# Who asks for the adapters: moving a layer's small loads from SyncE's queue to GpSimd's, and four row buffers used in turn

## The chip, the cores and the metric

The kernel runs on one core of a Trainium2 chip. Its metric is the device time of one execution in microseconds (us), taken as the median of several runs. The core has five engines with instruction streams of their own: TensorE (PE) multiplies and transposes, VectorE (DVE) and ScalarE (ACT) work element by element, GpSimd (POOL) and SyncE (SP) here mostly ask for transfers. Each stream runs in order; an instruction waits until its semaphores have the values that it names. A transfer is asked for by an engine's queue (SPq, POOLq, ACTq) and carried out by 16 DMA engines that all queues share.

## The reference

Four layers with residual connections follow each other on x, 64 sequences of 32 tokens of 512 features (2048 rows in all):

```python
x = x + L0(x, weight[ids0])                        # a 512x512 matrix chosen per sequence
x = x + (x @ W1.T + b1 + scale * (x @ A1[id].T) @ B1[id].T)   # 8 adapters of rank 16
x = x + (x @ W2.T + b2 + 2 * (x @ A2[id]) @ B2[id])           # 32 adapters of rank 16
x = x + attention(x)                               # QKV, norm, rope, paged cache, projection
```

All arithmetic is float32. The change touches only how the two middle lines (the low-rank layers) get their data.

## The kernel before

The stages run one behind another: layer 0, the two low-rank layers (`lora_layers`), QKV and attention, output projection. Every product is made in three passes over a high and a low part of each operand (L102 to L104), so each operand is split: ScalarE writes the high part, VectorE subtracts it to get the low part.

`lora_layers` holds the activations transposed (features on partitions). The 2048 rows are 16 tiles of 128 rows (`NT`), in four groups of four tiles (`LG`, `TPG`). Each of the two layers is applied to each group in a round; the eight rounds go in the order `ROUNDS` (layer, group): (0,0) (0,1) (1,0) (0,2) (1,1) (0,3) (1,2) (1,3). A round on TensorE is `low_rank` (the product with A), then four times `base` (with W) and `delta` (with B), one for each 128 output features. Ahead of each of the four `base` steps there may be one turn, four transposes of 128x128 (L798): in rounds 0, 2 and 4 an input tile of the next group ("x"), in rounds 3, 5 and 7 a finished tile ("z"), which ScalarE copies to a row buffer and SP stores.

A round of layer 1 needs the eight-sequence adapters of its group: for each half of a group, eight A matrices (128 partitions of 64 numbers, 32 KB) to `a_in` and eight B matrices (16 rows of 512 numbers, 32 KB) to `b_in`, each by a DMA of its own whose address comes from a register. That is 32 DMAs for a group. There is one `a_in` and one `b_in` buffer for each half, so a group's load has to wait until the group before has been split. The split of A is done one round ahead, at its head (`a_hi_part` on ScalarE, L654, then `a_lo_part` on VectorE, L741), before that round's additions (`add`, L728) on VectorE and their splits; that of B at the round's end (`b_hi_part` L662, `b_lo_part` L749).

SP asks for all of it in one written order: input tiles (`load_x`, L564), small constants, W2 (L592), the adapters (`load_adapters`, L576 and L578) and the stores (L583). In its loop over the groups the load of the adapters stands between the first two and the last two input tiles of a group:

```python
if g:
    sp.wait_ge(ab_split, 4 * g)
```

Input tile t goes to row buffer t for the first four tiles, then to buffer 0 or 1 alone (`x_buf`), since buffers 2 and 3 take the finished tiles. GpSimd does nothing in this stage.

Of the kernel before, what the change touches and what calls it, by code (L numbers as in the profile page):

```python
# [25 lines left out]
P = 128  # L26
NSEQ, SEQ, D = 64, 32, 512
TOK = NSEQ * SEQ
NT = TOK // P
SPT = P // SEQ  # L30
KC = D // P
NAD0 = 8
NAD1, NAD2, RANK = 8, 32, 16
# [423 lines left out]
LG = 4  # L457
GT = TOK // LG
TPG = NT // LG
HS = P // RANK  # L460
HT = HS * SEQ
ROUNDS = [(0, 0), (0, 1), (1, 0), (0, 2), (1, 1), (0, 3), (1, 2), (1, 3)]
ROUND_OF = {step: n for n, step in enumerate(ROUNDS)}
# [6 lines left out]
TURN_OF = {turn: n for n, turn in enumerate(TURNS)}  # L470


def lora_layers(nc, place, both, kept, a_in, b_in, weights_loaded, x_in, i, x_out, w_next):
# [9 lines left out]
    with ExitStack() as ctx:  # L483
        m = Mem(nc, ctx, "lora")
        w_hi, w_lo = low_part.sb("w_hi", [P, 2, KC, D], fp32r), low_part.sb("w_lo", [P, 2, KC, D], fp32r)
        state = [low_part.sb(f"state{n}", [P, KC, GT]) for n in range(2)] + [kept.w_stage[:, 1, :, :]]
# [8 lines left out]
        x_sb = high_part.sb("x", [P, 4, D])  # L495
        ids_f, ids2_sb = high_part.sb("ids_f", [P, NSEQ]), high_part.sb("ids2", [1, NSEQ], i32)
# [5 lines left out]
        small_loaded, ids2_loaded, mask_chain = m.sem("small_loaded"), m.sem("ids2_loaded"), m.sem("mask_chain")  # L502
        weights_hi, weights_split = m.sem("weights_hi"), m.sem("weights_split")
        x_loaded, turned = m.sems("x_loaded", 4), m.sem("turned")
        x_hi_done, x_split, z_copied = m.sem("x_hi_done"), m.sem("x_split"), m.sem("z_copied")
        ab_loaded, ab_hi_done, ab_split = m.sems("ab_loaded", 2), m.sem("ab_hi_done"), m.sem("ab_split")
        low_done, masked = m.sem("low_done"), m.sem("masked")
        low_hi_done, low_split = m.sem("low_hi_done"), m.sem("low_split")
        mm_done, y_ready, y_hi_done, y_split = m.sem("mm_done"), m.sem("y_ready"), m.sem("y_hi_done"), m.sem("y_split")
# [3 lines left out]
        A1, W1, B1, W2 = range(4)  # L513
        FIRST_OF = {A1: 0, W1: 1, B1: 1 + KC, W2: 2 + KC}
        PIECES_SPLIT = 2 + 2 * KC

        def pieces(which):
# [5 lines left out]
                return [(b_in[:, 1, :], b1_hi[:, :], b1_lo[:, :])]  # L523
            l = 0 if which == W1 else 1
            return [(w_in[:, l, k, :], w_hi[:, l, k, :], w_lo[:, l, k, :]) for k in range(KC)]

        def x_buf(t):
            return t if t < 4 else t % 2

        def x_loads(t):  # L530
            return 1 if t < 4 else (t - 4) // 2 + 2

        def tokens(g):
            return slice(g * GT, (g + 1) * GT)
# [1 line left out]
        def rows(t):  # L536
            return slice(t * P, (t + 1) * P)

        def in_group(t):
            return slice(t % TPG * P, (t % TPG + 1) * P)  # L540
# [12 lines left out]
        def adapters_after(n):  # L553

            step = ROUNDS[n + 1] if n + 1 < len(ROUNDS) else (0, 0)
            return step[1] if step[0] else None

        with nc.Block(no_gpsimd_drain=True) as block:
            @block.sync
            def _(sp):  # L560
                def load_x(t):
                    if t >= 4:
                        sp.wait_ge(turned, TURN_OF["x", t - 4 if t < 6 else t - 2] + 1)
                    sp.dma_start(x_sb[:, x_buf(t), :], x_in[rows(t), :]).then_inc(x_loaded[x_buf(t)], 16)  # L564

                def load_adapters(g):
                    for h in range(2):
                        _, adapters = nc.values_load_multi_w_load_instructions(
                            ids2_sb[0:1, (2 * g + h) * HS:(2 * g + h + 1) * HS], engines=[mybir.EngineType.SP],
                            min_val=0, max_val=NAD2 - 1, skip_runtime_bounds_check_because="ids are adapters")  # L570
                        if g:
                            sp.wait_ge(ab_split, 4 * g)
                        elif h:
                            sp.wait_ge(weights_split, FIRST_OF[W2])
                        for s, a in enumerate(adapters):
                            sp.dma_start(a_in[:, h, s * KC * RANK:(s + 1) * KC * RANK], i["a2"][bass.ds(a, 1)])\  # L576
                              .then_inc(ab_loaded[h], 16)
                            sp.dma_start(b_in[s * RANK:(s + 1) * RANK, h, :], i["b2"][bass.ds(a, 1)])\  # L578
                              .then_inc(ab_loaded[h], 16)

                def store(t):
                    sp.wait_ge(z_copied, t + 1)
                    sp.dma_start(x_out[rows(t), :], x_sb[:, 2 + t % 2, :]).then_inc(both.x_stored[t % 2], 16)  # L583

                for t in range(TPG):
                    load_x(t)
                for buf, src in smalls:
                    sp.dma_start(buf[:, :], src).then_inc(small_loaded, 16)
                sp.dma_start(ids2_sb[:, :], i["ids2"]).then_inc(ids2_loaded, 16)
                for t in range(TPG, TPG + 2):  # L590
                    load_x(t)
                sp.dma_start(w_in[:, 1, :, :], i["w2"]).then_inc(weights_loaded[W2], 16)  # L592
                sp.wait_ge(ids2_loaded, 16)
                load_adapters(0)
                for t in range(TPG + 2, TPG + 4):
                    load_x(t)
                sp.wait_ge(weights_split, FIRST_OF[B1])
                sp.dma_start(w_in[:, 0, :, :], w_next).then_inc(kept.w_loaded[0], 16)
                for g in range(1, LG):
                    if g < LG - 1:  # L600
                        for t in range(TPG * (g + 1), TPG * (g + 1) + 2):
                            load_x(t)
                    load_adapters(g)
                    if g < LG - 1:
                        for t in range(TPG * (g + 1) + 2, TPG * (g + 2)):
                            load_x(t)
                    for t in range(TPG * (g - 1), TPG * g):
                        store(t)
                for t in range(NT - TPG, NT):
                    store(t)  # L610

            @block.scalar
            def _(act):
# [33 lines left out]
                    act.activation(hi, state[g % 3][:, c, :], ACT.Copy).then_inc(y_hi_done, 1)  # L647

                def a_hi_part(g):
                    for h in range(2):  # L650
                        act.wait_ge(ab_loaded[h], 16 * 2 * HS * (g + 1))
                        if g:
                            act.wait_ge(low_done, ROUND_OF[1, g - 1] + 1)
                        act.activation(a2_hi[:, h, :, :].rearrange("p k (s r) -> p s k r", s=HS),  # L654
                                       a_in[:, h, :].rearrange("p (s k r) -> p s k r", s=HS, k=KC), ACT.Copy)\
                           .then_inc(ab_hi_done, 1)

                def b_hi_part(g):
                    if g:
                        act.wait_ge(mm_done, KC * (ROUND_OF[1, g - 1] + 1))  # L660
                    for h in range(2):
                        act.activation(b2_hi[:, h, :], b_in[:, h, :], ACT.Copy).then_inc(ab_hi_done, 1)  # L662
# [13 lines left out]
                for n in range(len(ROUNDS)):  # L676
                    g = adapters_after(n)
                    low_hi_part(n)
                    turn(n, 0)
                    if g is not None:  # L680
                        a_hi_part(g)
                    for c in range(KC):
                        y_hi_part(n, c)
                        if c + 1 < KC:
                            turn(n, c + 1)
                        if n == 0 and c == 0:
                            split_weights_hi(W2)
                    if g is not None:
                        b_hi_part(g)
# [96 lines left out]
            def _(pe):  # L786
                def transpose(kind, t):
                    turn = TURN_OF[kind, t]
                    if turn >= 2:
                        last_kind, last_t = TURNS[turn - 2]  # L790
                        pe.wait_ge(x_split if last_kind == "x" else z_copied, last_t + 1)
                    if kind == "x":
                        pe.wait_ge(x_loaded[x_buf(t)], 16 * x_loads(t))
                    else:
                        pe.wait_ge(y_ready, KC * (ROUND_OF[1, t // TPG] + 1))
                    for k in range(KC):
                        src = x_sb[:, x_buf(t), k * P:(k + 1) * P] if kind == "x" else state[t // TPG % 3][:, k, in_group(t)]
                        last = pe.transpose(ps_t[:, turn % 2, k, :], src, ident[:, :])  # L798
                    last.then_inc(turned, 1)

# [52 lines left out]
                def turn(n, at):  # L853
                    kind, t = turn_in(n, at)
                    if kind:
                        transpose(kind, t)

                pe.wait_ge(ident_ready, 1)
                for t in range(TPG):
                    transpose("x", t)  # L860
# [6 lines left out]
                for t in range(NT - TPG, NT):  # L867
                    transpose("z", t)
# [1127 lines left out]
```

## Time and profile before

| | |
|---|---|
| median of 3 runs | 2545.6 us (2545.35 to 2546.51) |
| profiled execution, its own time | 2544.21 us |
| its span, first to last instruction | 2542.6 us |
| mean granted TensorE clock | 0.976 |
| PE, DVE, ACT, POOL busy share of the span | 95%, 70%, 63%, 24% |
| low-rank stage, by the timeline | about 106 to 318 us |

The span is the length of the profiled execution without what lies ahead of its first and behind its last instruction, here 1.6 us. Times in the trace count from the start of the span. A busy share is a mean over stages that have different limits.

### The profile page before, as it was taken

To read this page: it belongs to the slowest core of one execution; us is meant where nothing else is said; L and a number is where in the kernel's file an instruction comes from. 1 tells how busy PE (TensorE), PEld (TensorE's weight loads), DVE (VectorE), ACT (ScalarE), POOL (GpSimd) and SP (SyncE) were. 2 spreads that over 40 slices of the span, in tenths; PEclk is the share of its full clock that TensorE was granted. 3 is DMA by queue.
4 is the path that set the end of the run, shared out by engine and by line. 5 is a ranking of instruction groups with operands and counts; after the bars stand their busy time and mean duration, and the time that the engine had idled before them with its cause. 6 is when DMAs were issued, how large, how long until landed. Compare 5 with 4: busy or idle time off the path is not lost. (4 is left out here: it accounts for less than half of the span.)

```text
span 2542.6 us, 54643 instructions
## 1 busy us (share of the span) xinstructions
PE 2409.0 (95%) x16070; PEld 2195.2 (86%) x16071; DVE 1780.3 (70%) x3632; ACT 1602.2 (63%) x3311; POOL 599.9 (24%) x896
## 2 busy tenths in 40 slices
PE   6878799999999979999999999999999997699999
PEld 4656688888888869999999999999999997588887
DVE  5434334989998977888878878788788884544443
ACT  3223235877777778888888888888888884311111
POOL 1200012000000024444444444444544442000000
PEclk9889999999999989999999999999999999799999
DMA  6521132333333469888888898888888884766664
GB/s 221 174 64 55 61 140 88 103 100 113 99 100 99 133 192 302 291 295 297 303 281 304 285 294 303 282 300 293 292 301 281 299 276 161 273 206 213 210 213 148
DMA packets 373752, 536.83 MB, mean 211 GB/s; under 512 B 49314, under 2 KB 263010, under 8 KB 369826
## 3 DMA queue, kind: packets, MB, share of 16 engines
q1 hardware_dynamic: 301538, 311.62, 38.2%
q0 software_dynamic: 70016, 221.30, 25.6%
q10 hardware_dynamic: 2112, 2.89, 0.4%
q8 instruction: 38, 0.62, 0.1%
q14 instruction: 48, 0.39, 0.0%
HBM read 437.35 MB, written 98.30 MB: 211 GB/s over the span
## 5 line engine op out<-in xcount | busy, mean ns | idle before, releaser
L1669 PE MATMUL both_ps_o<-att_pt,att_v 128*128 128x128 f32 x4096 | 539.3, 275 | 0.0
L1367 ACT ACTIVATE att_prob<-att_prob,att_shift 128x544 f32<-128x544 f32 x512 | 384.4, 751 | 205.5 <-DVE att_shift L1387 195.8
L1669 PEld LDWEIGHTS both_ps_o<-att_pt,att_v 128*128 128x128 f32 x4096 | 504.0, 191 | 0.0
L1387 DVE CUSTOM_DVE_ANT_0 att_prob<-both_ps_s,att_mask 128x544 f32<-128x544 f32 x512 | 365.0, 713 | 0.0
L102 PE MATMUL both_ps_s<-att_k_hi,att_q_hi 128*128 128x272 f32 x1024 | 339.2, 331 | 4.8 <-DVE att_k_lo L1362 4.8
L1362 DVE TENSOR_TENSOR att_k_lo<-att_k_raw,att_k_hi 128x1024 fp32r<-128x1024 f32 (+1 forms) x320 | 338.6, 1058 | 1.9 <-ACT att_k_hi L1356 1.9
L1646 PE MATMUL both_ps_pt<-both_ident,att_prob 128*128 128x128 f32 x2048 | 309.2, 274 | 7.8 <-ACT att_prob L1367 6.2
L104 PE MATMUL both_ps_s<-att_k_hi,att_q_lo 128*128 128x272 f32 x1024 | 298.0, 291 | 0.0
L1545 ACT ACTIVATE att_pt<-both_ps_pt 128x512 f32<-128x512 f32 x512 | 294.3, 575 | 2.2 <-PE both_ps_s L1654 1.2
L103 PE MATMUL both_ps_s<-att_k_lo,att_q_hi 128*128 128x272 f32 x1024 | 295.3, 288 | 0.0
L1356 ACT ACTIVATE att_k_hi<-att_k_raw 128x1024 fp32r<-128x1024 f32 (+1 forms) x320 | 292.7, 915 | 0.0
L1487 POOL DMA_INDIRECT att_v<-in_v_pages,att_rows_now x256 | 252.5, 986 | 86.1 <-issue 86.1
L1481 POOL DMA_DIRECT2D att_vo<-v_own x256 | 139.7, 546 | 555.1 <-PE both_ps_o L1672 494.0
L1577 DVE TENSOR_REDUCE att_p_own<-att_prob 128x32 f32<-128x32 f32 x512 | 91.0, 178 | 236.0 <-PE both_ps_s L104 222.0
L1646 PEld LDWEIGHTS both_ps_pt<-both_ident,att_prob 128*128 128x128 f32 x2048 | 242.4, 142 | 8.5 <-ACT att_prob L1367 6.5
L1823 ACT ACTIVATE out_o_hi<-out_o 128x2048 fp32r<-128x2048 f32 x32 | 61.4, 1918 | 290.3 <-DVE out_o L1850 282.5
L102 PE MATMUL out_ps_y<-out_w_hi,out_o_hi 128*128 128x512 f32 x512 | 202.9, 396 | 36.5 <-DVE out_w_lo L1843 31.0
L103 PE MATMUL out_ps_y<-out_w_lo,out_o_hi 128*128 128x512 f32 x512 | 202.1, 395 | 0.0
L104 PE MATMUL out_ps_y<-out_w_hi,out_o_lo 128*128 128x512 f32 x512 | 201.9, 394 | 0.0
L102 PEld LDWEIGHTS both_ps_s<-att_k_hi,att_q_hi 128*128 128x128 f32 x1024 | 194.7, 190 | 6.9 <-DVE att_k_lo L1362 5.2
L1672 PE MATMUL both_ps_o<-att_pto,att_vo 128*128 128x128 f32 x1024 | 198.0, 275 | 0.0
L103 PEld LDWEIGHTS both_ps_s<-att_k_lo,att_q_hi 128*128 128x128 f32 x1024 | 195.9, 191 | 0.0
(209 smaller groups left out, 5036.0 us busy)
## 6 DMA issues: line engine op xcount, KB each, us to landing
att_k_raw<-in_k_pages SPq DMA_DIRECT2D x1024, 128.0 KB, 4.8
q_t<-qkv_out_t SPq DMA_DIRECT2D x128, 256.0 KB, 2.3
att_q_raw<-q_t POOLq DMA_DIRECT2D x64, 512.0 KB, 7.5
o_t<-att_o POOLq DMA_DIRECT2D x64, 512.0 KB, 7.0
out_o<-o_t SPq DMA_DIRECT2D x32, 1024.0 KB, 6.0
out_inv<-inv_t SPq DMA_DIRECT2D x32, 1024.0 KB, 6.6
both_w_stage<-in_w_qkv SPq DMA_DIRECT2D x12, 1024.0 KB, 5.2
l_w_stage<-in_w SPq DMA_DIRECT2D x8, 1024.0 KB, 7.4
```

What stands on the lines that cost most here:

```text
L102: pe.matmul(out, xh, wh, start=start, stop=False)
L103: pe.matmul(out, xh, wl, start=False, stop=False)
L104: return pe.matmul(out, xl, wh, start=False, stop=stop)
L1356: act.activation(hi, raw, ACT.Copy).then_inc(hi_done, 1)
L1362: dve.tensor_tensor(lo, raw, f32(hi), ALU.subtract).then_inc(lo_done, 1)
L1367: act.activation(prob[:, b, :], prob[:, b, :], ACT.Exp, bias=shift[:, b:b + 1], scale=-1.0, accum_out=total[:, j // HK, j % HK:j % HK + 1] ...
L1387: dve.tensor_tensor_reduce(out=prob[:, b, :].rearrange("p (a n) -> p a n", a=2), in0=ps_s[:, j % 2, :, 0:HALF], in1=mask[:, j // HK, :].re ...
L1487: pool.indirect_dma_start(v_sb[p][:, c, :], None, v_pages.rearrange("n k x -> (n k) x"), bass.IndirectOffsetOnAxis(ap=rows_now[:, p, c:c + ...
L1545: act.activation(pt_sb[:, j % OG, :, :], ps_pt[:, j % 2, :, :], ACT.Copy).then_inc(pt_ready, 1)
L1646: mm = pe.transpose(ps_pt[:, j % 2, c, :], prob[:, j % NB_P, c * P:(c + 1) * P], ident[:, :])
L1669: pe.matmul(out, v_sb[p][:, c, h * DH:(h + 1) * DH], pt_sb[:, j % OG, c, :], start=(c == 0), stop=False)
L1672: pe.matmul(out, vo_sb[p][:, g % 2, j % OG, :], pto_sb[:, g % 2, :], start=False, stop=True).then_inc(pv_done, 1)
```

## The change

- The loads of the adapters go from SP's stream to GpSimd's. For a group they are in four lots: A of half 0, B of half 0, A of half 1, B of half 1, with eight DMAs in each.
- Each lot waits only for the split of what it overwrites: `ab_split` counts A0, A1, B0, B1 of a group, and the lots of group g wait for 1, 3, 2 and 4 of the group before. Before, both halves waited for all four.
- There is one semaphore for all A loads and one for all B loads. `a_hi_part` now waits ahead of its first half for all sixteen A loads of its group, and for no B load; `b_hi_part` waits for the B loads.
- Input tiles use all four row buffers in turn. Tile t waits until tile t-4 has been transposed. The last two (14 and 15) go to the buffers that finished tiles 0 to 3 have passed through and wait for those stores.
- On SP, W2 now stands behind input tiles 4 to 7; before, it stood behind 4 and 5. Tiles 8 to 11 are asked for before the first QKV weights.

```diff
-                        sp.wait_ge(turned, TURN_OF["x", t - 4 if t < 6 else t - 2] + 1)
-                    sp.dma_start(x_sb[:, x_buf(t), :], x_in[rows(t), :]).then_inc(x_loaded[x_buf(t)], 16)
+                        sp.wait_ge(turned, TURN_OF["x", t - 4] + 1)
+                    if t >= NT - 2:
+                        sp.wait_ge(both.x_stored[t % 2], 16 * 2)
+                    sp.dma_start(x_sb[:, t % 4, :], x_in[rows(t), :]).then_inc(x_loaded[t % 4], 16)
...
-                for t in range(TPG, TPG + 2):
+                for t in range(TPG, 2 * TPG):
                     load_x(t)
                 sp.dma_start(w_in[:, 1, :, :], i["w2"]).then_inc(weights_loaded[W2], 16)
-                sp.wait_ge(ids2_loaded, 16)
-                load_adapters(0)
-                for t in range(TPG + 2, TPG + 4):
+                for t in range(2 * TPG, 3 * TPG):
                     load_x(t)
                 sp.wait_ge(weights_split, FIRST_OF[B1])
                 sp.dma_start(w_in[:, 0, :, :], w_next).then_inc(kept.w_loaded[0], 16)
-                for g in range(1, LG):
-                    if g < LG - 1:
-                        for t in range(TPG * (g + 1), TPG * (g + 1) + 2):
-                            load_x(t)
-                    load_adapters(g)
-                    if g < LG - 1:
-                        for t in range(TPG * (g + 1) + 2, TPG * (g + 2)):
-                            load_x(t)
-                    for t in range(TPG * (g - 1), TPG * g):
-                        store(t)
+                for t in range(3 * TPG, NT - 2):
+                    load_x(t)
+                for t in range(TPG):
+                    store(t)
+                for t in range(NT - 2, NT):
+                    load_x(t)
+                for t in range(TPG, NT - TPG):
+                    store(t)
                 for t in range(NT - TPG, NT):
                     store(t)
+            @block.gpsimd
+            def _(pool):
+                def load_adapters(g):
+                    for h in range(2):
+                        _, adapters = nc.values_load_multi_w_load_instructions(
+                            ids2_sb[0:1, (2 * g + h) * HS:(2 * g + h + 1) * HS], engines=[mybir.EngineType.Pool],
+                            min_val=0, max_val=NAD2 - 1, skip_runtime_bounds_check_because="ids are adapters")
+                        if g:
+                            pool.wait_ge(ab_split, 4 * (g - 1) + h + 1)
+                        elif h:
+                            pool.wait_ge(weights_split, FIRST_OF[W2])
+                        for s, a in enumerate(adapters):
+                            pool.dma_start(a_in[:, h, s * KC * RANK:(s + 1) * KC * RANK], i["a2"][bass.ds(a, 1)])\
+                                .then_inc(a_loaded, 16)
+                        if g:
+                            pool.wait_ge(ab_split, 4 * (g - 1) + 2 + h + 1)
+                        for s, a in enumerate(adapters):
+                            pool.dma_start(b_in[s * RANK:(s + 1) * RANK, h, :], i["b2"][bass.ds(a, 1)])\
+                                .then_inc(b_loaded, 16)
+
+                pool.wait_ge(ids2_loaded, 16)
+                for g in range(LG):
+                    load_adapters(g)
...
                 def a_hi_part(g):
+                    act.wait_ge(a_loaded, 16 * 2 * HS * (g + 1))
+                    if g:
+                        act.wait_ge(low_done, ROUND_OF[1, g - 1] + 1)
                     for h in range(2):
-                        act.wait_ge(ab_loaded[h], 16 * 2 * HS * (g + 1))
...
                 def b_hi_part(g):
+                    act.wait_ge(b_loaded, 16 * 2 * HS * (g + 1))
```

## Rows read from the trace of the kernel before

**Rows 1.** Busy us by engine (x instructions) in the low-rank and the attention stage.
```profile
core 0: us, PE busy (x) PEld busy (x) DVE busy (x) ACT busy (x) POOL busy (x), PEclk, DMA share, GB/s
106.00:318.00 212.00, 162.41 (x800) 135.55 (x800) 84.21 (x125) 64.19 (x116) 0.00 (x0) 0.88 0.24 70
...
830.00:2260.00 1430.00, 1377.31 (x11193) 1342.44 (x11192) 1117.42 (x2517) 1101.93 (x2144) 551.47 (x835) 0.98 0.82 272
```

**Rows 2.** PE's timeline, turns only: start, duration, instruction, idle before and its releaser.
```profile
112.24 2.10 PE L798 MATMUL lora_ps_t<-both_ident,lora_x 128*128 128x128 f32 x8 [1.05 <-DVE both_xt_lo L703]
...
124.36 0.60 PE L798 MATMUL lora_ps_t<-both_ident,lora_x 128*128 128x128 f32 x4
...
133.91 1.08 PE L798 MATMUL lora_ps_t<-both_ident,lora_x 128*128 128x128 f32 x4 [5.46 <-DMA lora_x<-x]
...
140.47 0.60 PE L798 MATMUL lora_ps_t<-both_ident,lora_x 128*128 128x128 f32 x4
...
167.99 0.60 PE L798 MATMUL lora_ps_t<-both_ident,lora_x 128*128 128x128 f32 x4
...
184.28 1.09 PE L798 MATMUL lora_ps_t<-both_ident,lora_x 128*128 128x128 f32 x4 [12.20 <-DMA lora_x<-x]
...
189.69 0.60 PE L798 MATMUL lora_ps_t<-both_ident,lora_x 128*128 128x128 f32 x4
...
215.00 0.60 PE L798 MATMUL lora_ps_t<-both_ident,lora_x 128*128 128x128 f32 x4
...
218.94 0.60 PE L798 MATMUL lora_ps_t<-both_ident,lora_x 128*128 128x128 f32 x4
...
234.78 1.09 PE L798 MATMUL lora_ps_t<-both_ident,lora_x 128*128 128x128 f32 x4 [11.75 <-DMA lora_x<-x]
...
240.50 0.60 PE L798 MATMUL lora_ps_t<-both_ident,lora_x 128*128 128x128 f32 x4
...
293.10 1.08 PE L798 MATMUL lora_ps_t<-both_ident,both_w_stage 128*128 128x128 f32 x4 [4.09 <-DVE both_w_stage L728]
```

**Rows 3.** SP's timeline: W2, group 1's first adapter, input tiles 10 and 11.
```profile
111.64 0.43 SPq L592 DMA_DIRECT2D both_w_stage<-in_w  x1
...
164.87 0.34 SPq L576 DMA_DIRECT2D lora_a_in<-in_a  x1
...
181.44 0.88 SPq L564 DMA_DIRECT2D lora_x<-x  x2
```

**Rows 4.** ACT's timeline: the splits of W2 and of the adapters' A.
```profile
126.84 2.19 ACT L617 ACTIVATE lora_w_hi<-both_w_stage 128x512 fp32r<-128x512 f32 x4
...
148.60 1.14 ACT L654 ACTIVATE lora_a_hi<-lora_a_in 128x512 fp32r<-128x512 f32 x2
...
198.34 1.14 ACT L654 ACTIVATE lora_a_hi<-lora_a_in 128x512 fp32r<-128x512 f32 x2
...
284.79 0.63 ACT L654 ACTIVATE lora_a_hi<-lora_a_in 128x512 fp32r<-128x512 f32 x1 [8.07 <-DMA lora_b_in<-in_b]
```

**Rows 5.** DVE's timeline: B's split of groups 0 and 2, then the late addition.
```profile
163.42 1.29 DVE L749 TENSOR_TENSOR lora_b_lo<-lora_b_in,lora_b_hi 128x512 fp32r<-128x512 f32 x2
...
265.17 1.29 DVE L749 TENSOR_TENSOR lora_b_lo<-lora_b_in,lora_b_hi 128x512 fp32r<-128x512 f32 x2
...
286.06 0.74 DVE L728 SCALAR_TENSOR_TENSOR both_w_stage<-lora_ps_y,lora_bias,both_w_stage 128x512 f32<-128x512 f32 x1
```

**Rows 6.** POOL's DMA groups in the whole trace: total us, mean ns of one.
```profile
L1469 POOL DMA_DIRECT2D att_k_raw<-k_own x64 | 35.4, 553 | 57.7 <-DMA k_own<-qkv_out_t 57.5
...
L229 POOL DMA_DIRECT2D x<-l_y x44 | 22.0, 501 | 80.5 <-DVE l_y L390 78.8
```

**Rows 7.** POOL's timeline in layer 0: two stores, two register loads ahead of them.
```profile
58.41 1.08 POOL L229 DMA_DIRECT2D x<-l_y  x2 [1.33 <-DVE l_y L390]
```

**Rows 8.** DMA issues in three stretches: count, KB each, median us to landing.
```profile
both_w_stage<-in_w SPq DMA_DIRECT2D x1, 1024.0 KB, 8.8
...
lora_a_in<-in_a SPq DMA_DIRECT2D x16, 32.0 KB, 1.7
...
att_k_raw<-k_own POOLq DMA_DIRECT2D x1, 128.0 KB, 4.5
```

More of the change, by code:

```diff
@@ L505, in lora_layers @@
         x_hi_done, x_split, z_copied = m.sem("x_hi_done"), m.sem("x_split"), m.sem("z_copied")
-        ab_loaded, ab_hi_done, ab_split = m.sems("ab_loaded", 2), m.sem("ab_hi_done"), m.sem("ab_split")
+        a_loaded, b_loaded, ab_hi_done, ab_split = m.sem("a_loaded"), m.sem("b_loaded"), m.sem("ab_hi_done"), m.sem("ab_split")
         low_done, masked = m.sem("low_done"), m.sem("masked")
@@ L525, in pieces @@
             return [(w_in[:, l, k, :], w_hi[:, l, k, :], w_lo[:, l, k, :]) for k in range(KC)]
[L527 to L531, printed above, removed]
         def tokens(g):
@@ L562, in load_x @@
                     if t >= 4:
-                        sp.wait_ge(turned, TURN_OF["x", t - 4 if t < 6 else t - 2] + 1)
-                    sp.dma_start(x_sb[:, x_buf(t), :], x_in[rows(t), :]).then_inc(x_loaded[x_buf(t)], 16)
[L566 to L579, printed above, removed]
+                        sp.wait_ge(turned, TURN_OF["x", t - 4] + 1)
+                    if t >= NT - 2:
+                        sp.wait_ge(both.x_stored[t % 2], 16 * 2)
+                    sp.dma_start(x_sb[:, t % 4, :], x_in[rows(t), :]).then_inc(x_loaded[t % 4], 16)
                 def store(t):
@@ L649, in a_hi_part @@
                 def a_hi_part(g):
+                    act.wait_ge(a_loaded, 16 * 2 * HS * (g + 1))
+                    if g:
+                        act.wait_ge(low_done, ROUND_OF[1, g - 1] + 1)
                     for h in range(2):
-                        act.wait_ge(ab_loaded[h], 16 * 2 * HS * (g + 1))
-                        if g:
-                            act.wait_ge(low_done, ROUND_OF[1, g - 1] + 1)
                         act.activation(a2_hi[:, h, :, :].rearrange("p k (s r) -> p s k r", s=HS),
@@ L792, in transpose @@
                     if kind == "x":
-                        pe.wait_ge(x_loaded[x_buf(t)], 16 * x_loads(t))
+                        pe.wait_ge(x_loaded[t % 4], 16 * (t // 4 + 1))
                     else:
@@ L796, in transpose @@
                     for k in range(KC):
-                        src = x_sb[:, x_buf(t), k * P:(k + 1) * P] if kind == "x" else state[t // TPG % 3][:, k, in_group(t)]
+                        src = x_sb[:, t % 4, k * P:(k + 1) * P] if kind == "x" else state[t // TPG % 3][:, k, in_group(t)]
                         last = pe.transpose(ps_t[:, turn % 2, k, :], src, ident[:, :])
```

## The prediction

> **What bounds the kernel now.** I read the page first, then busy time by stage, then PE's timeline through the stage that the diff touches, and last SP, ACT and DVE around each gap found there. TensorE is busy for 95% of the span, but not in every stage: in the low-rank stage it works for 162.4 of 212 us, at a mean granted clock of 0.88 [rows 1]. So there are 50 us of idle time, and some work at the lower level of the clock (1.2 instead of 2.4 GHz). Only this stage can change; what comes behind it depends on its end and moves with it.
>
> PE's timeline shows where the time goes. Turns that find their tile ready come every 3.94 us (215.00 to 218.94). Three do not: tiles 6, 10 and 14, at 133.91, 184.28 and 234.78, each behind an idle time that the load of an input tile ends [rows 2]. SP's timeline says why: the first of group 1's 32 adapter DMAs goes out at 164.87, tile 10's load at 181.44 [rows 3]. SP spends 16.6 us on asking, and the tile stands behind it although its buffer was free earlier. A fourth gap has another form: the turn at 293.10 waits for an addition on VectorE [rows 2]. Round 6's additions start at 286.06 [rows 5], because the split of group 3's A stands ahead of them and the second half's arrives only at 284.79 [rows 4].
>
> **What goes: three stalls on input tiles.** I take start to start over two turns, so that the low clock after the stall is counted. At pace two turns need 7.88 us.
> - Tile 6: 140.47 - 124.36 - 7.88 = 8.2 us.
> - Tile 10: 189.69 - 167.99 - 7.88 = 13.8 us.
> - Tile 14: 240.50 - 218.94 - 7.88 = 13.7 us [rows 2].
>
> In each the idle time is 5.5, 12.2 and 11.8 us, the rest (2.6, 1.5, 1.8 us) is the turn and the base step behind it at the low clock: a turn lasts 1.08 us instead of 0.60 [rows 2]. What is late next? Without the stall of tile 6, the split of W2 (ACT from 126.84, 2.19 us [rows 4]) pushes tile 7's split to about 136.3, where the next low-rank product wants it at 136.15. I take off 0.2: 8.0 us. The other two leave nothing behind: their tiles are now loaded when tiles 6 and 7 are turned, some 30 us ahead, and, for 14 and 15, when the stores of tiles 2 and 3 have landed, near 191 on the new clock of the stage, against a need near 201. Sum: 8.0 + 13.8 + 13.7 = 35.5 us.
>
> **What is added: 128 DMAs on GpSimd's queue.** It is idle in this stage [rows 1], so the asking is free as long as the data comes in time. Three unknowns:
> - Spacing s of two DMAs. A 128-row load takes POOL 0.55 us, a 32-row store 0.50, and a pair of stores with register addresses 1.08 [rows 6, 7]. I take 0.62, with some register arithmetic. Bounds: 0.50 and, as on SP for A and B alike, 0.52 (16.6 / 32) are at the low end; at the high end I use 0.75, twice the arithmetic.
> - R, eight register loads. Two fit into 1.33 us of idle time [rows 7], so R is under 5.3; SP's whole lot of 16.6 us holds two such sets beside 32 DMAs, so it is likely under 1. I take 0.8, bound 2.
> - L, from asking to landing. SP's A load lands after 1.7 us; the one POOL load of 128 rows in a quiet stretch, four times as large, after 4.5 [rows 8]. I take 3.5, between these bounds and nearer to the POOL row.
>
> A sentence beside these: the Trainium skill ("DMA: Bandwidth & Descriptors", Latency and other measured facts) gives about 1 us to the first byte for a GpSimd DMA against 0.6 for SP's. By that alone L would be near 2.1 and the sum 1.4 us better; no row here shows it for this transfer.
>
> Each group wants its A before `a_hi_part`. The last A load is the sixteenth DMA counted from B0's start, which waits for the B0 split of the group before. So A is complete 15 s + R + L = 9.3 + 0.8 + 3.5 = 13.6 us after that split.
> - Group 0: POOL starts near 113.5 (W2's request at 111.64 [rows 3] and a small load's landing); 23 s + 2 R + L = 19.4 us later it is 132.9. Wanted at 148.60 - 8.0 = 140.6 [rows 4]. Hidden by 7.7.
> - Group 1: the split ends at 163.42 + 0.65 - 8.0 = 156.1 [rows 5]; wanted at 198.34 - 21.8 = 176.5 [rows 4]. Budget 20.4 against 13.6. Hidden by 6.8. Group 2 has the same distances.
> - Group 3: here there is no round between. The split ends at 265.17 + 0.65 = 265.8 [rows 5], A is complete at about 279.5 (old clock of the stage), and ACT has long been waiting. From the split's start to the first addition are then 1.9 us, both halves in a row. So the addition comes at 281.4 instead of 286.06 [rows 5]: 4.7 us gained, and the turn at 293.10 moves with it. PE still idles over 4 us there, so I count no gain of clock.
>
> The B loads end eight DMAs later and are wanted a round later: hidden.
>
> **What moves.** W2 is asked for behind tiles 6 and 7, which wait for the turns of tiles 2 and 3 (until 114.3 [rows 2]): some 3 us later than 111.64. It took 8.8 us [rows 8], so it lands near 123.6, with half a megabyte more ahead of it perhaps 124.5; its split starts at 126.84 [rows 4]. Hidden by 2 us; if that cover goes, each microsecond costs one. Tiles 14 and 15 behind stores, and stores behind tile loads, cost nothing (above; ACT waits for a store only two tiles on).
>
> **Sum.** 35.5 + 4.7 = 40.2 us. The profiled execution took 2544.2 us (span 2542.6), 1.4 below the median of 2545.6. It would take 2504.0; the median 2505.4. I say 2505.5. All tests below use 5 us (0.2%) as what a measurement of this kernel tells from no change.
>
> **The rivals.**
> 1. *The last gap closes further.* POOL is quick (s 0.54, R 0.6, L 1.7): A of group 3 arrives 10.4 us after the split instead of 13.6, 3.2 us more gained, and PE's idle time there may be too short for the clock to fall, 1.7 more. Gain 45, time 2500.5. For it: the pair of 1.08. Against it: the 4.5 us. It is inside my range; 0.08 for gains beyond 44.
> 2. *POOL's DMAs wait for VectorE.* The mechanism: a DMA on POOL cannot go on while a VectorE operation runs. VectorE makes 125 operations in 84.2 us here [rows 1], 0.67 us each. If each DMA waits for a whole one, s = 1.29. Then group 0's A (23 s) is late beyond s = 0.96 and groups 1 and 2 (15 s) beyond 1.07, so the gain is 103.7 - 68 s = 16 us, the time about 2529.5. Against it: in the attention stage VectorE is busy for 1117 of 1430 us [rows 1] and POOL's loads still take 0.55 [rows 6]. I give 0.06. The Trainium skill ("SBUF — State Buffer", Who interferes with whom) states a rule of this kind: a VectorE instruction with two SBUF inputs keeps out a GpSimd one that reads SBUF, for its whole length. The subtractions of L736 and L749 are of that form; by the attention stage's rows the trace does not show it for DMAs.
> 3. *POOL becomes the bound (the other side).* The same sum reaches zero at s = 1.53: all four groups' A late, group 0 by 13 us, groups 1 and 2 by 7 each, group 3's gain turned into a loss of 9. Then slower than before above s = 1.6; at s = 1.8 the time is 2564. It needs a DMA to cost three times what any direct POOL row shows; many small pieces (A has 128 of 256 bytes) would be the reason. 0.04.
> 4. *The change doesn't reach what PE waits for:* tiles 6, 10 and 14 are late for another reason, such as the shared DMA engines being full. They are busy for 0.24 of the stage [rows 1]. Time 2545.6. 0.02.
>
> **How the numbers follow.** Forecast (gain 33 to 44): 0.80; rival 1 0.08, rival 2 0.06, rival 3 0.04, rival 4 0.02. The forecast's own ends: the slow ends of s, R and L together (0.75, 2, 4.5) put A of group 3 at 17.8 us after the split, 4.2 later than taken, and W2 late by 2 more makes 6: 2511.5. The quick ends make 2500.5. With the small rest of rival 2 the range of 8 in 10 is 2499 to 2514. Faster by over 0.2%: 0.94; within: 0.02; slower: 0.04.
>
> **What the new profile would show.** Turns of tiles 6, 10 and 14 without idle time and 0.60 us long; PE's busy time in the stage near 157 us in a stretch of 172. SP with single tile loads right behind the turns. POOL with lots of eight DMAs; their spacing is s, the last A of group 3 to ACT's L654 is L. ACT's L654 waiting in group 3 alone. The turn of tile 8's result still behind idle time that VectorE ends. The prediction is wrong if L654 waits in group 0, 1 or 2 (s over 0.96), if VectorE's operations grow longer beside POOL's DMAs, if the W2 split (L617) waits, or if a tile turn waits for a load again.

## The result, and the profile after

| | before | after |
|---|---|---|
| median of 4 runs | 2546.06 us (2545.35 to 2548.94) | 2504.11 us (2501.86 to 2507.69) |
| profiled execution, its span | 2544.21, 2542.6 us | 2502.53, 2501.0 us |
| ratio | | 0.9834, 95% interval 0.9817 to 0.9851 |

The forecast was 2505.5 us, with 2499 to 2514 as its range; 2504.1 lies 1.4 below it. The span is 41.6 us shorter.

The windows view of the kernel after, in the low-rank stage (the columns are those of [rows 1]):
```profile
106.00:276.40 170.40, 155.79 (x800) 130.36 (x800) 83.82 (x124) 63.29 (x115) 65.77 (x128) 0.94 0.28 87
```
It answers to the first of [rows 1]. The stage ends 41 us sooner with the same 800 matmuls. PE is busy for 6.6 us less, since fewer of them ran at the low clock (mean 0.94 instead of 0.88), and POOL now works for 65.8 us.

PE's timeline of the kernel after, turns of tiles 5, 6, 7, 10, 11, 14, 15 and of tile 8's result:
```profile
125.90 0.60 PE L800 MATMUL lora_ps_t<-both_ident,lora_x 128*128 128x128 f32 x4
129.84 0.60 PE L800 MATMUL lora_ps_t<-both_ident,lora_x 128*128 128x128 f32 x4
133.78 0.60 PE L800 MATMUL lora_ps_t<-both_ident,lora_x 128*128 128x128 f32 x4
...
165.37 0.60 PE L800 MATMUL lora_ps_t<-both_ident,lora_x 128*128 128x128 f32 x4
169.32 0.60 PE L800 MATMUL lora_ps_t<-both_ident,lora_x 128*128 128x128 f32 x4
...
202.51 0.60 PE L800 MATMUL lora_ps_t<-both_ident,lora_x 128*128 128x128 f32 x4
206.46 0.60 PE L800 MATMUL lora_ps_t<-both_ident,lora_x 128*128 128x128 f32 x4
...
252.25 1.08 PE L800 MATMUL lora_ps_t<-both_ident,both_w_stage 128*128 128x128 f32 x4 [3.40 <-DVE both_w_stage L730]
```
The idle times of 5.46, 12.20 and 11.75 us before tiles 6, 10 and 14 [rows 2] are gone: these turns come 3.94 us behind the one before and last 0.60 us. Against the same turns of [rows 2], tile 7's is 6.7 us earlier (140.47 to 133.78), tile 11's 20.4, tile 15's 34.0, and that of tile 8's result 40.9 (293.10 to 252.25). So the three stalls and the last gap gave 6.7, 13.7, 13.7 and 6.8 us. The remaining 0.7 us of the span lie behind that turn, 0.3 of them still in this stage.

The last gap is smaller but there. ACT's timeline of the kernel after, the splits of W2 and of group 3's A:
```profile
128.38 2.19 ACT L618 ACTIVATE lora_w_hi<-both_w_stage 128x512 fp32r<-128x512 f32 x4
...
243.32 1.15 ACT L655 ACTIVATE lora_a_hi<-lora_a_in 128x512 fp32r<-128x512 f32 x2 [9.61 <-DMA lora_a_in<-in_a]
```
DVE's, the split of group 2's B and the first addition of round 6:
```profile
231.16 1.29 DVE L751 TENSOR_TENSOR lora_b_lo<-lora_b_in,lora_b_hi 128x512 fp32r<-128x512 f32 x2
...
245.20 0.75 DVE L730 SCALAR_TENSOR_TENSOR both_w_stage<-lora_ps_y,lora_bias,both_w_stage 128x512 f32<-128x512 f32 x1
```
POOL's, the lots B0 and A1 of group 3 between them:
```profile
232.13 4.06 POOL L606 DMA_DIRECT2D lora_b_in<-in_b  x8 [10.39 <-DVE lora_b_lo L751]
237.21 4.63 POOL L601 DMA_DIRECT2D lora_a_in<-in_a  x8 [1.02 <-issue]
```
ScalarE waits 9.6 us for A. The lot B0 waits for VectorE's split, A1 waits behind B0, ScalarE for A1, and the additions stand behind the split. From the first half of the B split (231.8) to the addition it is 13.4 us; before it was 20.2 [rows 5].

### The profile page after: what moved, and what is told of

It is laid out like the page before. It is cut to its first block and busy times, and to the rows that moved or that the text cites. A ratio compares the mean times of both kernels' runs of the same rounds, so it can differ in the third digit from the quotient of the medians.

```text
span 2501.0 us, 54645 instructions
## 1 busy us (share of the span) xinstructions
PE 2403.6 (96%) x16070; PEld 2190.7 (88%) x16071; DVE 1779.8 (71%) x3632; ACT 1601.7 (64%) x3311; POOL 663.3 (27%) x1024
```

## The experiments

The kernels ran in three batches, each batch on one chip beside the kernel before. Medians in us:

| batch | kernel | median | less than before |
|---|---|---|---|
| 1 | before | 2641.6 | |
| 1 | r_after, the changed kernel | 2601.6 | 40.0 |
| 1 | e_sp_asks | 2600.8 | 40.8 |
| 1 | e_two_bufs | 2600.5 | 41.1 |
| 1 | e_order_only | 2607.3 | 34.3 |
| 2 | before | 2547.2 | |
| 2 | e_a_first | 2499.0 | 48.2 |
| 2 | e_sp_a_first | 2497.2 | 50.0 |
| 2 | e_cut2 | 2519.8 | 27.4 |
| 2 | e_cut4 | 2665.8 | -118.6 |
| 3 | before | 2547.4 | |
| 3 | r_after2, the changed kernel | 2504.3 | 43.1 |
| 3 | e_wait_all | 2509.7 | 37.6 |
| 3 | e_two_bufs_w2 | 2511.7 | 35.6 |
| 3 | e_sp_a_first2 | 2498.4 | 49.0 |

The executions of one kernel in a batch spread over 1.4 to 6 us (11.6 in e_sp_a_first), so differences of medians under 2 us say nothing. Batch 1's chip is slower for every kernel; the expectations' absolute times are those of the other two chips, so there the last column is to be compared (the changed kernel's is 40 to 43). One of the six executions of e_two_bufs took 7369.7 us, which no row explains; it doesn't matter to the median.

**The base lines, r_after and r_after2.** The changed kernel, unedited.

> The changed kernel once more, as the base line of this chip for the runs beside it. Both theories: 2504 us (measured 2504.1).

> The changed kernel, as the base line of this chip for the runs beside it: 2504 us where the kernel before takes 2546.

It gains 40.0 and 43.1 us: ratios 0.9846 (0.9833 to 0.9858) and 0.9833 (0.982 to 0.9847).

**Is it GpSimd's queue, or the order? e_sp_asks.** GpSimd's block goes; SP gets the same lots with the same waits. The function `load_adapters`, which goes over with SP in GpSimd's place, is left out here:
```diff
+                sp.wait_ge(ids2_loaded, 16)
+                load_adapters(0)
                 for t in range(2 * TPG, 3 * TPG):
                     load_x(t)
...
+                load_adapters(1)
                 for t in range(3 * TPG, NT - 2):
                     load_x(t)
                 for t in range(TPG):
                     store(t)
                 for t in range(NT - 2, NT):
                     load_x(t)
+                load_adapters(2)
                 for t in range(TPG, 2 * TPG):
                     store(t)
+                load_adapters(3)
                 for t in range(2 * TPG, NT - TPG):
                     store(t)
...
-            @block.gpsimd
...
```


> The changed kernel, but SP asks for the adapters again, in the new order: each group's adapters behind the input tiles that are wanted before them, in lots A0, B0, A1, B1, with the new waits and four row buffers. Theory 1 (TensorE waited only for the place of the tile loads in one queue; any queue that brings the data in time will do): no tile turn waits; group 3's A is complete 8 + 0.8 + 1.7 = about 10.5 us after the B split (SP's spacing of about 0.5), against 11.5 on GpSimd: 2503 us, within 2 of the changed kernel. Theory 2 (a queue of its own for the adapters is what helps; SP cannot carry both in time): at least one tile turn waits again or a store holds the copies up, 5 to 25 us more: 2509 to 2530.

The same time within noise, 0.9 us below r_after. SP's timeline, group 3's lots A0, B0 and A1:
```profile
228.78 4.00 SPq L572 DMA_DIRECT2D lora_a_in<-in_a  x8
232.90 3.90 SPq L577 DMA_DIRECT2D lora_b_in<-in_b  x8
237.53 3.99 SPq L572 DMA_DIRECT2D lora_a_in<-in_a  x8
```
SP asks every 0.5 us, no slower than GpSimd, and no tile turn waits. Theory 2 falls: GpSimd's queue is one way to get the order, and not needed for it.

**The order alone, in the kernel before: e_order_only.** Two row buffers, one queue, the wait for all four splits.
```diff
-                sp.wait_ge(ids2_loaded, 16)
-                load_adapters(0)
                 for t in range(TPG + 2, TPG + 4):
                     load_x(t)
+                sp.wait_ge(ids2_loaded, 16)
+                load_adapters(0)
...
-                        for t in range(TPG * (g + 1), TPG * (g + 1) + 2):
+                        for t in range(TPG * (g + 1), TPG * (g + 2)):
                             load_x(t)
                     load_adapters(g)
-                    if g < LG - 1:
-                        for t in range(TPG * (g + 1) + 2, TPG * (g + 2)):
-                            load_x(t)
```


> The kernel before with one edit: the four input tiles of a group are asked for ahead of the adapters in SP's order; two buffers, SP alone, the wait for all four splits. Theory 1: tiles 6, 10 and 14 no longer wait (35.5 us gained), but SP waits for the turn of the fourth tile before it starts on the adapters, so the A of groups 0, 1 and 2 comes about 2 us later than ScalarE wants it (5 to 7 us in all if nothing covers it), and group 3's gap stays: 2546 - 29 = 2517 us, 2510 to 2520. Theory 2 (a queue of its own is needed): little gained, over 2530.

34.3 of the 40.0 us, where I had expected 29. ACT's timeline of this run, A's second half in groups 0, 1, 2 and 3:
```profile
144.18 0.63 ACT L651 ACTIVATE lora_a_hi<-lora_a_in 128x512 fp32r<-128x512 f32 x1 [3.06 <-DMA lora_b_in<-in_b]
...
180.88 0.63 ACT L651 ACTIVATE lora_a_hi<-lora_a_in 128x512 fp32r<-128x512 f32 x1 [3.84 <-DMA lora_b_in<-in_b]
...
217.07 0.63 ACT L651 ACTIVATE lora_a_hi<-lora_a_in 128x512 fp32r<-128x512 f32 x1 [2.89 <-DMA lora_b_in<-in_b]
...
249.27 0.63 ACT L651 ACTIVATE lora_a_hi<-lora_a_in 128x512 fp32r<-128x512 f32 x1 [8.11 <-DMA lora_b_in<-in_b]
```
In this kernel one semaphore counts the A and the B loads of a half, so the split of A waits for both. In groups 0 to 2 they are late by 2.9 to 3.8 us, as thought, but PE has no idle time in those rounds: it goes on in the open round meanwhile. A wait of ScalarE is not yet a wait of TensorE. Group 3's gap stays whole: PE idles 4.81 us ahead of the last low-rank product and 3.98 ahead of the turn of tile 8's result, where the kernel before idles 4.80 and 4.09 and the changed kernel only 3.49 in all (r_after, on the same chip). That is the difference to the changed kernel.

**Are the four buffers needed? e_two_bufs and e_two_bufs_w2.** Both use the old buffers for input tiles. The first also has W2 back ahead of tiles 6 and 7; the second leaves it behind them: of the diff it has only the first part, up to the first "...". The two functions for the buffer numbers and the reading side on PE, both as in the kernel before, are left out.
```diff
-                        sp.wait_ge(turned, TURN_OF["x", t - 4] + 1)
-                    if t >= NT - 2:
-                        sp.wait_ge(both.x_stored[t % 2], 16 * 2)
-                    sp.dma_start(x_sb[:, t % 4, :], x_in[rows(t), :]).then_inc(x_loaded[t % 4], 16)
+                        sp.wait_ge(turned, TURN_OF["x", t - 4 if t < 6 else t - 2] + 1)
+                    sp.dma_start(x_sb[:, x_buf(t), :], x_in[rows(t), :]).then_inc(x_loaded[x_buf(t)], 16)
...
-                for t in range(TPG, 2 * TPG):
+                for t in range(TPG, TPG + 2):
                     load_x(t)
                 sp.dma_start(w_in[:, 1, :, :], i["w2"]).then_inc(weights_loaded[W2], 16)
-                for t in range(2 * TPG, 3 * TPG):
+                for t in range(TPG + 2, 3 * TPG):
                     load_x(t)
...
```


> The changed kernel, but input tiles from tile 4 on use row buffers 0 and 1 alone, as before, with W2 asked for ahead of tiles 6 and 7. GpSimd asks for the adapters. Theory 1: with SP free a tile is asked for at the turn of the tile two ahead, 7.9 us before its own turn, and lands in 3: no wait, 2504 us, within 2 of the changed kernel. Theory 3 (the four buffers carry part of the gain): tile turns wait, 5 us or more: over 2509.

> As e_two_bufs (input tiles in two row buffers, GpSimd asks for the adapters), but W2 stands behind tiles 6 and 7, as in the changed kernel. Tile 7 now waits for the turn of tile 5, so W2 is asked for near 126.5 and lands near 134, where ScalarE wants it at 128.4. Theory (as the prediction says: its cover is about 2 us, beyond it each microsecond costs one; in the trace of the changed kernel tile 7's split ends 0.06 us before the low-rank product wants it): 5.5 us, perhaps with some low clock: 2509 to 2512 us. Rival (a late W2 is covered by TensorE's open round): 2504 to 2506.

PE's timeline of e_two_bufs, turns of tiles 6 and 7:
```profile
130.14 0.60 PE L804 MATMUL lora_ps_t<-both_ident,lora_x 128*128 128x128 f32 x4
134.07 0.60 PE L804 MATMUL lora_ps_t<-both_ident,lora_x 128*128 128x128 f32 x4
```
Nothing waits; two buffers do while the adapters are out of the tiles' way. With W2 behind tile 7 it costs 7.4 us against r_after2. SP's, ACT's and PE's timelines of e_two_bufs_w2:
```profile
126.50 1.79 SPq L577 DMA_DIRECT2D both_w_stage<-in_w  x1
```
```profile
133.58 2.20 ACT L622 ACTIVATE lora_w_hi<-both_w_stage 128x512 fp32r<-128x512 f32 x4 [5.48 <-DMA both_w_stage<-in_w]
```
```profile
142.83 0.80 PE L102 MATMUL lora_ps_low<-both_xt_hi,lora_a_hi 128*128 128x512 f32 x1 [5.38 <-DVE both_xt_lo L709]
```
ScalarE waits 5.48 us for W2, and the next low-rank product 5.38: one for one. Most of the rest is the low clock behind it: this product takes 4.2 us here, 2.9 in the changed kernel, and its first matmul lasts 0.80 us. What the four buffers carry in this change is W2's new place.

**The finer waits: e_wait_all.**
```diff
                         if g:
-                            pool.wait_ge(ab_split, 4 * (g - 1) + h + 1)
+                            pool.wait_ge(ab_split, 4 * g)
...
-                        if g:
-                            pool.wait_ge(ab_split, 4 * (g - 1) + 2 + h + 1)
```


> The changed kernel, but GpSimd starts on a group's adapters only when all four splits of the group before are done, as SP did, and then asks without a further wait. Theory 1: groups 1 and 2 have A complete about 17 us after the B split, in a budget of 20: hidden. In group 3 the A0 lot now stands behind the wait too: 8 DMAs of 0.58 and the second B split (0.6) more, 5 to 6 us later: 2509 to 2510 us. Rival (the finer waits bring nothing, since the B split ends the wait in any case): 2504.

5.4 us above r_after2. ACT's timeline, group 3's A:
```profile
247.93 1.15 ACT L653 ACTIVATE lora_a_hi<-lora_a_in 128x512 fp32r<-128x512 f32 x2 [15.24 <-DMA lora_a_in<-in_a]
```
ScalarE waits 15.2 us instead of 9.6, 5.6 more; the earlier groups don't wait. The finer waits thus bring 5.6 of the 6.8 us that the change gains in the last gap (from tile 15's turn to that of tile 8's result: 52.6 us before, 51.4 here, 45.8 after). What brings the other 1.2 us was not tried by itself. One difference that is left is the order of the DMAs: the kernel before asks for A and B of a half in turn, so the last A is nearly the last of 32; here A1 goes ahead of B1.

**The rest of the last gap: e_a_first and e_sp_a_first.** The lots go A0, A1, B0, B1, so A1 no longer stands behind the wait of B0; from GpSimd, and from SP in the order of e_sp_asks. `ids(h)` reads the numbers of the eight adapters of half h into registers; it runs ahead of each lot.
```diff
                     for h in range(2):
...
                         for s, a in enumerate(adapters):
                             pool.dma_start(a_in[:, h, s * KC * RANK:(s + 1) * KC * RANK], i["a2"][bass.ds(a, 1)])\
                                 .then_inc(a_loaded, 16)
+                    for h in range(2):
+                        adapters = ids(h)
                         if g:
                             pool.wait_ge(ab_split, 4 * (g - 1) + 2 + h + 1)
                         for s, a in enumerate(adapters):
                             pool.dma_start(b_in[s * RANK:(s + 1) * RANK, h, :], i["b2"][bass.ds(a, 1)])\
                                 .then_inc(b_loaded, 16)
```


> The changed kernel, but GpSimd asks for a group's adapters in the order A0, A1, B0, B1 (the register loads repeated for the B lots). In the changed kernel A1 stands behind B0, which waits for the B split of the group before; A's own buffers are free 15 us earlier. Theory 1 (the last gap is group 3's A behind that wait): ScalarE's split of A does not wait in group 3, the turn of tile 8's result does not wait, and the low clock behind it goes too: 4.97 us from start to start, 2499 us. Rival (B takes its place: complete at the B split + 8.2 + 0.8 + 2.0 = 11 us, wanted at about 13; or the additions are the limit anyway): 2503 to 2505.

> As e_a_first, but SP asks for everything, in the order of e_sp_asks; GpSimd does nothing in the stage. Theory 1: 2499 us, the same as e_a_first. Theory 2 (SP cannot carry both): 5 us or more above e_a_first.

> The version with A first and SP asking for everything, once more beside the changed kernel on one chip, as its difference decides whether it beats it: 5 us less than r_after2 by the trace (4.97 us from start to start), 2499.

ACT's timeline of e_a_first, group 3's A, and PE's, the turns of the results of tiles 8 and 9:
```profile
233.65 1.14 ACT L659 ACTIVATE lora_a_hi<-lora_a_in 128x512 fp32r<-128x512 f32 x2
```
```profile
248.69 0.60 PE L804 MATMUL lora_ps_t<-both_ident,both_w_stage 128*128 128x128 f32 x4
252.63 0.60 PE L804 MATMUL lora_ps_t<-both_ident,both_w_stage 128*128 128x128 f32 x4
```
No wait is left on either, and the turns come at pace. On its chip e_a_first takes 2499.0, as expected. e_sp_a_first takes 2497.2 there and 2498.4 beside the changed kernel's 2504.3: 5.9 us less. The intervals of the ratios to the kernel before (0.9797 to 0.9824 against 0.982 to 0.9847) just overlap, while the five times of each kernel don't (2498.25 to 2500.52 against 2501.95 to 2505.64); the trace, with the idle time gone, is the firmer evidence. This version beats both kernels and leaves GpSimd free.

**GpSimd as the bound: e_cut2 and e_cut4.** Each adapter DMA in 2 or 4 pieces of fewer rows (CUT); the same is done for B, and the two waits on ScalarE count CUT times as much.
```diff
-                            pool.dma_start(a_in[:, h, s * KC * RANK:(s + 1) * KC * RANK], i["a2"][bass.ds(a, 1)])\
-                                .then_inc(a_loaded, 16)
+                            for q in range(CUT):
+                                at = slice(q * P // CUT, (q + 1) * P // CUT)
+                                pool.dma_start(a_in[at, h, s * KC * RANK:(s + 1) * KC * RANK],
+                                               i["a2"][bass.ds(a, 1), at, :]).then_inc(a_loaded, 16)
...
```


> The changed kernel, each adapter DMA cut into two of half the rows: 256 DMAs on GpSimd. Theory 1 (the price is by DMA, 0.5 to 0.58 us each in the trace of the changed kernel, whatever its rows, and what counts is when A is complete): A complete 8.2 + 0.8 + 8.8 + 2.0 = 19.8 us after the B split instead of 11.5. Groups 1 and 2 have 20.0 and stay hidden, group 0 is about 1 us late and is covered, group 3 loses 8.3 one for one: 2512 us. Rival A (the price is by row): no change, 2504. Rival B (no cover at all for a late A, as the prediction counted it): 2514 and waits in group 0.

> The changed kernel, each adapter DMA cut into four: 512 DMAs on GpSimd. This tests the forecast's rival on the other side (GpSimd as the bound), as if one DMA cost four times as much. Theory 1: A of group 0 about 26 us late, of groups 1 and 2 16 us each, of group 3 25 us later than now. About 6 us of lateness is covered for groups 0 to 2, since TensorE can go on in the open round: 20 + 10 + 10 + 25 = 65 us and some low clock, 2570 to 2580, slower than the kernel before. By the prediction's own formula without cover, 92 us: about 2596. Rival A (price by row): 2504.

POOL's timeline of e_cut2, group 0's B1, group 1's A0 and the start of group 3's B0, and PE's first wait behind the start of the stage, for group 3's A:
```profile
142.00 8.15 POOL L611 DMA_DIRECT2D lora_b_in<-in_b  x16
151.15 9.27 POOL L604 DMA_DIRECT2D lora_a_in<-in_a  x16 [1.00 <-issue]
...
237.83 2.55 POOL L611 DMA_DIRECT2D lora_b_in<-in_b  x5
```
```profile
259.12 0.55 PE L102 MATMUL lora_ps_low<-lora_y_hi,lora_a_hi 128*128 128x256 f32 x1 [13.05 <-DVE lora_a_lo L748]
```
The windows view of e_cut4 over its stage, and PE's longest wait there, for group 3's A:
```profile
106.00:434.00 328.00, 174.97 (x800) 145.03 (x800) 83.43 (x124) 63.62 (x114) 257.49 (x512) 0.74 0.15 44
```
```profile
395.20 0.55 PE L102 MATMUL lora_ps_low<-lora_y_hi,lora_a_hi 128*128 128x256 f32 x1 [40.91 <-DVE lora_a_lo L748]
```
The price is by DMA: a piece of half the rows takes as long. But both runs are slower than expected, 2519.8 against 2512 and 2665.8 against 2570 to 2580. I had counted each group from its B split on, as if GpSimd were free by then. In e_cut2 group 1's A0 starts at 151.15, though its buffer is free from about 144.6: GpSimd still asked for group 0's B1 until 150.2. The first lots of groups 2 and 3 start 8.3 and 6.2 us behind the release of their buffers too (in group 2 with 3.4 us of idle time among them, for which the profile shows no cause). In group 3 the B0 lot starts at 237.83, 6.0 us behind the B split at 231.9, and all of it is paid: A is complete near 257.6, 25.7 us after the split where I expected 19.8. Against the changed kernel (243.32) that is 14.3 us later; the run gains 15.7 us less than r_after2 does. In groups 0 to 2 ScalarE waits 1.1, 4.2 and 5.7 us for A, and PE not at all. In e_cut4 GpSimd asks from 112.7 to 408.5 us with no pause over 3.1, 257 us of it in the DMAs themselves, and PE waits eight times for more than 4 us.

## Why the prediction was right, step by step

- **The cause.** Tiles 6, 10 and 14 waited for their place in SP's order. Shown three ways: the waits are gone in the new trace, the order alone gives 34.3 of 40.0 us, and SP with the new order gives all of it. Rival 4 falls.
- **The three stalls, 35.5 us.** 13.7 and 13.7 us came as predicted for tiles 10 and 14. Tile 6 gave 6.7 instead of 8.0. The stall itself did give 8.2: tile 7's turn is 7.88 us behind tile 5's, where it was 16.1. But tile 5's turn is 1.5 us later than before: the stage's first low-rank product starts 0.4 us later, and PE's timeline shows a low clock that lasts longer in it, first before, then after:
```profile
118.96 0.47 PE L102 MATMUL lora_ps_low<-both_xt_hi,lora_a_hi 128*128 128x512 f32 x1
```
```profile
120.63 0.63 PE L102 MATMUL lora_ps_low<-both_xt_hi,lora_a_hi 128*128 128x512 f32 x1
```
  From this product's start to tile 4's turn it is 4.2 us before and 5.3 after. That is no cost of the change: the same changed kernel takes 5.3 us in r_after's trace and 4.9 in r_after2's, and e_wait_all, whose edit touches nothing ahead of group 1, takes 4.2 as before. It differs from execution to execution. The 0.2 us that I took off did not arise, but only just: tile 7's split ends 0.06 us before it is wanted. In the prediction the shares of the low clock in the three stalls (2.6, 1.5 and 1.8 us) should read 2.8, 1.6 and 1.9 by its own rows; nothing rests on them, as the sum goes from start to start.
- **The last gap, 4.7 us.** The mechanism was right, the terms were too dear: it gave 6.8. POOL's groups in the stage, mean ns of one, and the landing times of A and of W2:
```profile
L601 POOL DMA_DIRECT2D lora_a_in<-in_a x64 | 34.5, 540 | 43.7 <-DVE lora_a_lo L743 28.2 <-issue 13.1
L606 POOL DMA_DIRECT2D lora_b_in<-in_b x64 | 31.3, 489 | 32.2 <-DVE lora_b_lo L751 29.9 <-issue 1.2
```
```profile
lora_a_in<-in_a POOLq DMA_DIRECT2D x64, 32.0 KB, 2.0
...
both_w_stage<-in_w SPq DMA_DIRECT2D x1, 1024.0 KB, 7.7
```
  Spacing was 0.58 for A and 0.51 for B instead of 0.62, the register loads 1.0 instead of 0.8, and landing 2.0 instead of 3.5: A complete 11.5 us after the split instead of 13.6. The largest miss is L: I leaned on a POOL load four times as large (4.5 us [rows 8]), and SP's 1.7 for the very same transfer was nearer. The misses of -1.3 us at tile 6 and +2.1 us here have opposite signs, so part of the closeness of 2505.5 to 2504.1 is luck. The Trainium skill's difference of 0.4 us to the first byte ("DMA: Bandwidth & Descriptors", Latency and other measured facts) gave 2.1; the trace, with 2.0, agrees.
- **The cover of groups 0 to 2 and of W2.** Right: neither wait appears, VectorE's operations are no longer than before (0.68 against 0.67 us on average), and none of the other signs of being wrong is there. PE is busy for 155.8 us in a stretch of 170.4, where I had said 157 in 172. W2 lands about 122.8 (asked for at 115.12) and is split from 128.38, 5.6 us later; I had put 2. Beyond the cover a microsecond costs one, as e_two_bufs_w2 shows, and the low clock comes on top.
- **Rival 1** came more than halfway on the POOL side: A was complete 11.5 us after the split, between my 13.6 and its 10.4. But PE still idled 3.4 us and the clock still fell (the turn at 252.25 lasts 1.08 us), so its last 1.7 us did not come. e_a_first then shows what lay behind it.
- **Rival 2** falls: GpSimd's DMAs did not take longer beside VectorE's operations. The tile view of `lora_a_in`, nanoseconds min/median/max of one, first and last start in us:
```profile
L601 POOL DMA_DIRECT2D lora_a_in<-in_a x64: 534/534/573, 113.5 to 241.3; - x64
```
  None of the 64 is longer by even a tenth of a VectorE operation (0.69 us). A wait could also stand between two DMAs of a lot. There are six such pauses in the stage, of 0.16 to 1.05 us, and the profile puts none down to VectorE; they are in the idle times above, and a spacing near the rival's 1.29 us is ruled out. The rule of the Trainium skill ("SBUF — State Buffer", Who interferes with whom) on VectorE instructions with two SBUF inputs and GpSimd ones that read SBUF does not reach these DMAs; as far as this trace shows, asking for them is not such an instruction.
- **Rival 3, the formula.** Its kind was right (with enough work GpSimd is the bound and the kernel slower, e_cut4), its formula wrong in two opposite ways. It charged each late A to TensorE in full, while lateness of 3 to 4 us in groups 0 to 2 (e_order_only), and up to 5.7 (e_cut2), cost nothing. And it let each group start on time, while a full queue starts late (e_cut2). For four times the DMAs, at the measured spacing of 0.545 us on average, it gives 103.7 - 68 x 2.18, a loss of about 44 us; 119 were measured.

## What to carry to other kernels

Before a stream of small loads is moved to another queue, look at what stands behind it in the old one: here the place of three tile loads was worth 34 us, and either queue could have given it. Ask for each lot when its own buffer is free, and put first the lots that are wanted first and wait for the least; a lot without a wait must not stand behind one with a wait. For the question how much a queue can still take, follow it from lot to lot and not only from a release to a need: a lot that is still being asked for when the next could start delays it. In e_cut2 this cost 6 us in the last group, although all its DMAs together take 131 us, less than the stage.

## What the runs showed of the hardware

- Asking for a DMA from GpSimd cost 0.49 to 0.54 us, whether it had 128, 64, 32, 16 or 4 rows; on SP with lots of one kind it is as much (0.50 from start to start).
- Behind each idle time of PE in the last gap the low clock followed, but not always at once. Behind 3.40 us the turn itself lasted 1.08 us instead of 0.60. Behind 2.67 us, in e_sp_asks, the turn lasted 0.63, and the matmuls behind it were slow, 0.63 us instead of 0.39; PE's timeline of that run:
```profile
252.12 0.63 PE L801 MATMUL lora_ps_t<-both_ident,both_w_stage 128*128 128x128 f32 x4 [2.67 <-DVE both_w_stage L731]
...
254.14 0.63 PE L103 MATMUL lora_ps_y<-lora_y_lo,lora_w_hi 128*128 128x512 f32 x1
```
- Batch 1's chip took 94 us more for the kernel before and 97 more for the changed one. The windows view of the attention stage, first r_after there, then the changed kernel's first profile:
```profile
790.00:2310.00 1520.00, 1394.26 (x11166) 1338.25 (x11165) 1109.16 (x2513) 1100.49 (x2143) 547.42 (x835) 0.98 0.77 256
```
```profile
790.00:2218.00 1428.00, 1376.81 (x11183) 1342.02 (x11182) 1116.05 (x2514) 1100.73 (x2142) 549.07 (x835) 0.98 0.82 272
```
  The same work takes 92 us longer at the same granted clock; the low-rank stage, from its first turn to its last, is the same within 0.3 us. The bytes are the same too, so the lower rate (256 instead of 272 GB/s) says no more than that the stage is longer. Why it is longer on this chip was not tried. It means that only kernels of one chip are compared.
